# Second attention of a Perceiver kernel by pairs of positions, with a transposed down projection and another order of loads

## The reference

```
x += xattn0(ln(x), ctx, bias)        # 16 heads of 16, over 1024 keys, then a GELU MLP
x += delta_memory(ln(x))             # chunked recurrence with a 64x64 inverse
x += sum over 8 experts of silu(x Wg) * (x Wu) @ Wd
x += xattn1(ln(x), ctx)              # below
x += attn1(ln(x))                    # 16 heads of 16 within the 64 positions
x += top-1 of 8 relu experts
```

```
q = x @ Wq; k, v = split(context @ Wkv)
mask = (j % n_q == i)                # n_q = 64 positions: key j counts only for query j % 64
attn = softmax(where(mask, q k^T / 8, -max))
out = (attn @ v) @ Wout + bout
```

## Time and profile before

| what | value |
|---|---|
| median of 3 executions | 916.06 us |
| the profiled execution's own time | 919.98 us |
| its span (first to last instruction) | 918.2 us |
| mean granted clock | 0.975 |
| TensorE busy | 855.8 us, 93% |
| VectorE busy | 508.3 us, 55% |
| ScalarE busy | 412.6 us, 45% |
| GpSimd busy | 105.6 us, 12% |
| DMA | 128.15 MB, 139 GB/s from and to HBM |

### The profile page before, as it was taken

The page is one execution under the profiler, slowest core; times in us unless marked ns, Lnnn a source line. Parts: engine busy times, 40 slices in busy tenths (PEclk is TensorE's granted clock), DMA queues, the critical chain, the costliest instruction groups (busy, mean ns, idle before and its releaser), DMA issues.

```text
span 918.2 us, 20804 instructions
## 1 busy us (share of the span) xinstructions
PE 855.8 (93%) x8290; PEld 709.5 (77%) x8290; DVE 508.3 (55%) x1182; ACT 412.6 (45%) x820; POOL 105.6 (12%) x102
## 2 busy tenths in 40 slices
PE   5999999999799799999999999999989999659997
PEld 3788888888657787888888888884489957547786
DVE  4778887787616646555555555544366504734232
ACT  3666666666631224545454545442456522401221
POOL 2333332130000700000000000000011003100100
PEclk9999999999999899999999999999999999778999
DMA  8446664464360000302312321009046594040960
GB/s 301 174 154 204 226 221 179 173 203 152 132 259 0 3 4 0 138 18 121 138 51 87 137 88 49 0 0 353 13 145 267 184 380 171 2 185 14 372 260 24
DMA packets 25868, 128.15 MB, mean 140 GB/s; under 512 B 2360, under 2 KB 8272, under 8 KB 21712
## 3 DMA queue, kind: packets, MB, share of 16 engines
q1 hardware_dynamic: 24624, 111.51, 32.6%
q0 software_dynamic: 1184, 15.77, 4.4%
HBM read 126.75 MB, written 0.52 MB: 139 GB/s over the span
## 4 chain that ended last, share of the span: by engine, by line
PE 85%; DVE 7%; DMA 3%; issue 2%; ACT 2%; SPq 0%; DVEq 0%; ACTq 0%
PE PS L387 13%; PE PS L388 13%; PE PS L389 13%; PE PS L698 5%; PE PS L396 4%; PE PS L940 4%; PE PS L1142 3%; PE PS L821 3%; PE PS L959 3%; PE PS L710 3%; PE PS L687 3%; PE PS L1154 3%; DMA arena<-in_bias 2%; PE PS L928 2%; PE PS L913 2%
## 5 line engine op out<-in xcount | busy, mean ns | idle before, releaser
L1679 DVE TENSOR_TENSOR w_l<-arena,w_h 128x768 fp32r<-128x768 f32 x64 | 61.2, 957 | 91.6 <-ACT w_h L1322 91.6
L1322 ACT CAST w_h<-arena 128x768 fp32r<-128x768 f32 x64 | 53.4, 836 | 129.2 <-PE PS L389 129.2
L387 PE MATMUL PS<-xnT_h,w_h 128*128 128x512 f32 x256 | 100.5, 393 | 0.8 <-DVE xnT_l L381 0.8
L388 PE MATMUL PS<-xnT_l,w_h 128*128 128x512 f32 x256 | 100.3, 392 | 0.0
L389 PE MATMUL PS<-xnT_h,w_l 128*128 128x512 f32 x256 | 99.6, 389 | 0.0
L1517 DVE CUSTOM_DVE_ANT_0 arena<-PS,arena 128x512 f32<-128x512 f32 x128 | 86.7, 714 | 19.6 <-PE PS L687 17.9
L1222 ACT ACTIVATE arena<-arena 128x1024 f32<-128x1024 f32 x64 | 73.5, 1151 | 10.7 <-DVE arena L1517 10.6
L389 PE MATMUL PS<-w_h,h_l 128*128 128x256 f32 x256 | 72.4, 283 | 0.0
L388 PE MATMUL PS<-w_l,h_h 128*128 128x256 f32 x256 | 72.4, 283 | 0.0
L387 PE MATMUL PS<-w_h,h_h 128*128 128x256 f32 x256 | 72.1, 282 | 0.0
L698 PE MATMUL PS<-consts,arena 128*128 128x128 f32 x512 | 68.3, 277 | 0.7 <-ACT arena L1227 0.4
(11 more groups left out here) (297 smaller groups left out, 1832.1 us busy)
## 6 DMA issues: line engine op xcount, KB each, us to landing
arena<-in_bias SPq DMA_DIRECT2D x64, 512.0 KB, 4.1
arena<-in_wall SPq DMA_DIRECT2D x8, 3072.0 KB, 10.2
arena<-in_wf SPq DMA_DIRECT2D x8, 2052.0 KB, 11.4
hT<-in_ctxT SPq DMA_DIRECT2D x12, 1024.0 KB, 6.5
arena<-in_ctxT SPq DMA_DIRECT2D x4, 1024.0 KB, 6.4
arena<-in_ctxG SPq DMA_DIRECT2D x4, 1024.0 KB, 4.8
hT<-in_ctxG SPq DMA_DIRECT2D x4, 1024.0 KB, 4.8
arena<-in_w SPq DMA_DIRECT2D x2, 1024.0 KB, 6.3
```

The source lines that it names most:

```text
L387: pe.matmul(out, a[0], b[0], start=start, stop=False)
L388: pe.matmul(out, a[0], b[1], start=False, stop=False)
L1322: act.copy(w_h[:, s % 4, :], stage[s // 8 % 2][:, s % 8, :]).then_inc(sem("c_wh"), 1)
L1679: dve.tensor_tensor(w_l[:, s % 4, :], stage[s // 8 % 2][:, s % 8, :], wide(w_h[:, s % 4, :]), ALU.subtract).then_inc(sem("c_wl"), 1)
```

## The change

Three parts.

1. **Second attention two positions at a time.** U becomes `U[dc]` = [batch x pair of positions, 2 x 16 heads], so a pair's 32 columns lie side by side. Scores of a pair are [32 columns] x [32 keys], placed in one of four 32-column groups of the array; 4 pairs in parallel groups, 8 such steps fill [128, 256] of one bank. The regrouping copies go. DVE adds the constant "pair" (0 or -1e30), takes the maximum and subtracts it for all 8 steps at once, ACT takes one exponential, DVE sums and normalises. Two transposes instead of eight. The sums run on 32-row groups, one per pair, each into a bank of its own (4 to 7). Scores and sums of a batch have two buffers in PSUM where they had halves, the results' banks have one. Loops over batches are written out.
2. **Down projection of the first layer's experts turned around.** The weights are the stationary operand, the result is channels x tokens in banks 4 and 5; DVE and ACT copy it to `aT`, TensorE transposes it into banks 6 and 7, and DVE adds it.
3. **SP queue.** wq1, wkT1 and wv1 are loaded during the experts; wqkv, wproj and the second layer's experts 0 to 4 together after L982's last product (`d_o`); wrt and b2f ahead of experts 6 and 7. The context in the new layouts `ctxD` and `ctxG` is loaded in the order T, G for each batch; T of batch b waits for the scores of b - 2, G for the sums of b - 2, as before.

More of the change, by code:

```diff
@@ L46, in const_layout @@
         "half2": ((p % 32) // DK == np.arange(2)[None, :]),
-        "group": np.where(p % GI == c % GI, 0.0, -BIG),
+        "pair": np.where(p % 2 == np.arange(32)[None, :] % 2, 0.0, -BIG),
         "upper": i > j,
@@ L464, in _ @@
             sp.wait_ge(sem("a2_o"), 2)
-            with sp.Fori(0, NEXP // 2) as i:
+            for e2 in range(2):
+                sp.dma_start(stage[e2], A["wall"][e2:e2 + 1].rearrange("a p c n -> p (a c) n"))\
+                  .then_inc(sem(f"c_w{e2}"), 16)
+            with sp.Fori(1, NEXP // 2) as i:
                 for e2 in range(2):
@@ L476, in _ @@
             w_in(wv1, A["wv1"], "in_wvo1")
+            sp.wait_ge(sem("c_dn"), 4 + 8 * NEXP)
             w_in(wo1, A["wo1"], "in_wvo1")
[L478 to L490, removed]
+            for b in range(B):
+                if b >= 2:
+                    sp.wait_ge(sem("d_sim"), b - 1)
+                sp.dma_start(ctxT1[b % 2], A["ctxD"][b].rearrange("(k p) n -> p k n", p=P))\
+                  .then_inc(sem(f"d_ctxT{b % 2}"), 16)
+                if b >= 2:
+                    sp.wait_ge(sem("d_w"), b - 1)
+                sp.dma_start(ctxG[b % 2], A["ctxG"][b]).then_inc(sem(f"d_ctxG{b % 2}"), 16)
+            sp.wait_ge(sem("d_o"), FC)
             w_in(wqkv, A["wqkv"], "in_wqkv")
@@ L495, in expert_in @@
                 sp.dma_start(wblk[e], A["wf"][e * P:(e + 1) * P]).then_inc(sem(f"f_w{e // 2}"), 16)
[L497 to L501, removed]
+            for e in range(5):
                 expert_in(e)
@@ L929, in _ @@
                                   start=True, stop=True).then_inc(sem(f"d_u{dc}"), 1)
[L931 to L955, removed]
-                    for dc in range(KC):
[L957 to L962, removed]
@@ L1362, in exps @@
             def exps(b):
-                for hf in range(2):
-                    act.wait_ge(sem("d_z"), b * 2 + hf + 3)
-                    for g in range(4):
-                        last = act.activation(Z[:, hf, g, :], Z[:, hf, g, :], ACT.Exp, bias=mx1[:, hf, g:g + 1],
-                                              scale=-1.0, accum_out=rs1[:, hf, g:g + 1])
-                    last.then_inc(sem("d_e"), 1)
+                act.wait_ge(sem("d_z"), b + 1)
+                z = Z[:, b % 2].rearrange("p a b -> p (a b)")
@@ L1370, in transposed @@
+                act.activation(z, z, ACT.Exp).then_inc(sem("d_e"), 1)
             def transposed(b):
[L1371 to L1373 removed]
+                act.wait_ge(sem("d_t"), b + 1)
+                act.copy(PTx[:, b % 2].rearrange("p a b -> p (a b)"), PS[:, 2 + b % 2, 0:2 * P])\
+                   .then_inc(sem("d_te"), 1)
@@ L1375, in summed @@
             def summed(b):
-                for hf in range(2):
-                    act.wait_ge(sem("d_w"), b * 4 + hf * 2 + 7)
-                    act.copy(U[:, 1, :, bass.ds(b * S + hf * 32, 32)].rearrange("p h (g i) -> p g h i", g=4),
-                             PS[:, 5 + 2 * hf, :].rearrange("p (g h i) -> p g h i", g=4, h=XH))\
-                       .then_inc(sem("d_we1"), 1)
-            exps(0)
-            with act.Fori(1, B) as b:
-                transposed(b - 1)
-                exps(b)
-                summed(b - 1)
@@ L1387, in _ @@
-            transposed(B - 1)
-            summed(B - 1)
+                act.wait_ge(sem("d_w"), b + 1)
+                for dc in range(KC):
+                    last = act.copy(U[dc][:, b * PP + 16:(b + 1) * PP, :].rearrange("p (r q) n -> p r (q n)", r=2),
+                                    PS[:, 6:8, dc * D:(dc + 1) * D])
+                last.then_inc(sem("d_we1"), 1)
+            exps(0)
+            for b in range(B):
+                transposed(b)
+                if b + 1 < B:
+                    exps(b + 1)
+                summed(b)
@@ L1700, in _ @@
             dve.wait_ge(sem("c_dn"), 4 + 8 * NEXP)
-            for t in range(NT):
-                ch.add(dve.tensor_tensor(x_tok[:, t, :], PS[:, 4 + t, 0:D], x_tok[:, t, :], ALU.add))
+            dve.tensor_copy(aT[:, 0], bank(4)).then_inc(sem("c_turn"), 1)
+            for i in range(2):
+                dve.wait_ge(sem("c_y"), i + 1)
+                ch.step(dve.tensor_tensor(two(x_tok, i), bank(6 + i), two(x_tok, i), ALU.add))
+                ln_stats(dve, ch, x_tok, (2 * i, 2 * i + 1))
             ch.sync()
             dve.sem_inc(sem("x_tok"), 1)
-            ln_stats(dve, ch, x_tok, range(NT))
             ln_dve(dve, ch, 6, x_tok, xn_tok, sem("tr_src"))
@@ L1751, in _ @@
             scores(0)
-            grouped(1)
             probabilities(0)
-            with dve.Fori(1, B - 1) as b:
-                ch.enter(b - 1, 2)
-                scores(b)
-                grouped(b + 1)
-                probabilities(b)
-                summed(b - 1)
-                ch.leave(B - 2)
-            scores(B - 1)
-            probabilities(B - 1)
-            summed(B - 2)
-            summed(B - 1)
+            for b in range(B):
+                if b + 1 < B:
+                    scores(b + 1)
+                    probabilities(b + 1)
+                summed(b)
```

116 lines of the change are left out of this document (40 added, 76 removed).

## The result

The changed kernel takes 924.05 us (median of 6, 919.12 to 927.42) against 914.34 for the kernel before (median of 6): ratio 1.0105, interval 1.0069 to 1.014. Run once more beside the last experiments it was 918.14 against 914.15, ratio 1.0048, interval 1.0026 to 1.0071. It is slower, by half to one per cent; the forecast was faster by 3%.

What follows compares the result with a forecast made beforehand. TensorE, busy 93% of the span, was taken to bound the kernel. Terms -3.5 + 2.4 - 16.1 - 13.8 = -31.0 from the median of 916.06 gave 885 us; own range 878 to 892, wider range 871 to 914.

Steps and rivals of the forecast that it cites:

- the attention's round: Second attention, TensorE's time per batch: scores 2.1, transposes and handovers 1.2, sums 3.6, tiling change 0.1; 7.0 us against 8.5.
- the serial rival: Second attention's sums: row groups load weights one after another, 14.3 us instead of 3.6; kernel 970 us, chance 0.05.
- The rival had the falling clock: Second attention's loop: clock falls to 1.2 GHz for few columns in flight and pauses; round 11.1, kernel 914 us, chance 0.14.
- Instruction supply: Second attention's scores: supply of instructions sets the time, 2.1 us for 128 records.
- The rival had it as a slower rate: Second attention's scores: slower instruction supply, 3.5 us, round 8.4; kernel 895 us, chance 0.15.
- the second 7.2 us after the trigger: Second attention's context loads: ctxT, queued behind ctxG, lands 7.2 us after sums end and gates scores one round later.
- The rule (7.0 + 7.2)/2: Second attention: round is the larger of TensorE's 7.0 us and the mean with the transfers' 7.2, so 7.1 us.
- Pair reading in the `wv1` products: Products after the second attention: reading the moving operand in pairs costs 0; bounds 0 and 13.97 us.
- The rival of halved speed (+14): Products with `wv1`: pairs halve TensorE's read, + 14 us; kernel 899 us, chance 0.08.
- Down projection: First layer's expert blocks: 6 records of 512 columns replace 12 of 256, -3.5 us over 64 blocks; bounds 0 and -7.
- The transposes behind it: After the experts' last product: copies and transposes before the adds and statistics, 5.3 us against 2.96, +2.4 us.
- Router: Router: early input loads remove waiting, -8.2 us, and the clock stays at 1.0, 5.6 us more; -13.8 in all.

Runs made afterwards that it cites:

- fill: Changed kernel plus unused full-array matmuls in the second attention, 2 or 6 a batch: 920.54 us (2) and 915.63 us (6).
- wide resident loop: Changed kernel, 128 columns streamed in sums, up to 64 in scores, transposes ahead of next scores, six middle batches as a two-batch loop: 892.98 us, ratio 0.978.
- no pauses: Changed kernel with each batch's transposes issued ahead of the next batch's scores: 916.11 us, ratio 1.0015 to the kernel before.
- narrow: Changed kernel, 32 columns streamed, transposes ahead of next scores, TensorE's six middle batches as a two-batch loop: 908.08 us, ratio 0.9932 to the kernel before.
- wide without pauses: Changed kernel, sums streaming 128 columns and scores up to 64 instead of 32, transposes ahead of next scores: 909.03 us, ratio 0.9946 to the kernel before.
- the last kernel: The wide resident loop with ctxT of batch b + 1 issued ahead of ctxG of batch b: 885.70 us, ratio 0.9695 to the kernel before.
- attention undone: Changed kernel's projection and router order, with the attention, contexts and loads of the kernel before: 894.02 us, ratio 0.9774.

## Why the prediction was wrong

**The step that failed** is the attention's round, "2.1 + 1.2 + 3.6 + 0.1 = 7.0 us against 8.5". It took sums of 3.6 us from rows at 2.4 GHz and left the clock at 1.0. The size is right for that clock: 3.84 with fill, 3.75 to 3.77 in the wide resident loop, so the four row groups do load side by side (the serial rival is excluded). At the granted 0.5 they take 7.05 or more, and the sums of the eight batches are 26 of the 31.6 us by which the loop missed. Another 4 us went before the first sums, 10.3 us behind the first scores where 6.0 was forecast, with a stop of 2.57 us in them.

The rival had the falling clock and even the size of a round (11.1 against 10.7 to 11.6). Of its two reasons one stands, the few columns in flight; the pauses that it named as well are not needed for it. I gave it 0.14 because "small-tile matmuls without pause kept 1.00" from 313 to 333. That row is another kind of matmul, 692 records of 64x64 tiles with 64 columns streamed, and "no pauses" shows that pauses are not the point: TensorE without one stays at 0.50, and comes up once each instruction drives more columns (0.84) or full-array work stands between (0.82). The narrow and the wide resident loop differ in nothing but the columns streamed, and have 0.59 and 0.89. I should have asked how much work each instruction puts into the array, not how busy the engine is called. That this is how the chip decides isn't shown; the runs show which streams were held down and which came up.

On that, the Trainium skill (TensorE: Matmul & The Clock Gate, "Why this matters for your kernels") advises to leave no long idle gaps between bursts of matmuls. By this case's runs that is not enough: "no pauses" has none of more than about half a microsecond from 667 us on and stays at 1.2 GHz.

**Instruction supply.** I priced it as a rate: 2.1 us for 128 scores, from L1019. As a rate that was high, it is 1.82 (0.0142 a record; at the low clock 1.75 for 116, 0.0151, so the clock hardly sets it). The rival had it as a slower rate, 3.5 us; it has the rate wrong, but supply does cost, as stops of some 2 us at every 512 instructions. In the changed kernel they are short (0.3 to 1.1 us a batch), as is to be expected where the low clock slows what uses the instructions up. With the clock up they are the next limit: wide without pauses, with a clock of 0.84, is at 909.

The Trainium skill (Runtime: NRT & Kernel Launch, "Instruction fetch mechanics") has the 16 KB blocks of 256 instructions that the trace shows, and holds that their fetch is hidden since the sequencer dispatches more slowly than it fills; it prefers full unrolling, because a taken branch can break the prefetch. Here an unrolled stream of small matmuls is stopped all the same, and a loop of two batches is 15 us faster (wide: 0.9946 to 0.978).

**Transfers.** "the second 7.2 us after the trigger" is right (6.8 to 6.9 to land, plus issue). The rule (7.0 + 7.2)/2 was hidden by the slow round. In the wide resident kernel, whose TensorE round is 5.9, it gives (5.9 + 7.2)/2 = 6.55, and the chain has scores waiting for ctxT at 697.89 and, two batches on, at 710.88: 6.5 us a batch. The other order of the queue removes it.

**Pair reading in the `wv1` products.** Forecast 0 loss. At full clock the 64 records take 15.79 us, with fill and in the last kernel alike, against 13.97: +1.8 us, 13%. In the changed kernel it is 17.40, since the clock is back only at about 759; that is the other 1.6 of the stage's +3.4. The rival of halved speed (+14) is out. The pairs are what the change does to these products, and the loads that ran beside them before are gone; no run undoes the pairs alone. The Trainium skill (SBUF — State Buffer, "Door 1: The DMA port swizzle") has full bandwidth from two accesses to a 16-byte line on, and also a penalty, of no stated size, at each step to a new line; the prediction took the first half alone. Measured, pairs are 13% slower.

**Down projection.** -3.5 forecast, -6.3 measured; right in kind. After, the six records of a block step by 0.2265 us:

```profile
...
512.63 0.39 PE L386 MATMUL PS<-h_h,w_h 128*128 128x512 f32 x1
...
513.99 0.39 PE L386 MATMUL PS<-xnT_h,w_h 128*128 128x512 f32 x1
...
516.71 0.39 PE L386 MATMUL PS<-h_h,w_h 128*128 128x512 f32 x1
...
```

They take 1.36 us where 12 took 1.43, and the gate and up products 2.72 where 2.75 was: 0.10 x 64 = 6.4. I had counted the saving on the down part alone. The transposes behind it cost +1.9, forecast +2.4. The last record of the products starts at 622.57; the copy, the first add and the last statistics follow:

```profile
...
622.99 0.69 DVE L1677 COPY aT<-PS 128x512 f32<-128x512 f32 x1 [1.94 <-PE PS L388]
...
624.89 0.69 DVE L1680 TENSOR_TENSOR x_tok<-PS,x_tok 128x512 f32<-128x512 f32 x1 [1.20 <-PE PS L878]
...
626.99 0.75 DVE L317 BATCH_NORM_STATS2 small<-x_tok 128x6 f32<-128x256 f32 x2
...
```

From the copy to the end of the statistics 4.75 us; forecast were 5.3 with 0.1 ahead of it, before it was 2.96.

**Router.** -8.2 and -5.6 forecast, -6.8 to -8.3 and -5.7 measured. Not forecast were -4.6 at the end: before, TensorE stops in the L1142 blocks for 0.34 to 0.38 us at a time, as here, and these stops are gone in every kernel with the new order, also where that order is the only edit.

```profile
...
847.61 0.39 PE PS L1142 x6
848.00 0.34 issue
848.34 0.39 PE PS L1142 x6
848.73 0.34 issue
...
```

What makes them isn't shown.

**Before the experts.** Their first product starts at 352.9 us in the profile of before and 361.5 after, but 357.8 in the changed kernel's second profile and 351.5 to 355.7 in the experiments that kept the new contexts and have the same code up to there. (The expectation of "attention undone" reads this start some 3 us later, at 356 and 365.) So the 8.6 us are no certain cost of the change. In the chain up to there, the landing of a bias tile (`in_bias`, 512 KB) stands twice before, 15.8 us in all, and six times in both profiles of the changed kernel, 48 us; in the kernel "wide, no pauses", which starts at 351.5, three times. Why these loads are waited for more often isn't shown.

The sum: parts 2 and 3 gave what was forecast and 5 us more (894.02 against a forecast of 899 for them alone, 914.34 - 3.5 + 2.4 - 13.8), and part 1 turned from -16 into +19 in its own stages (query stage, loop and `wv1` products), +25 to +30 with the later start before the experts. That the last kernel comes to 885.70, the number once forecast for the changed one, is in part luck: its loop takes 63.5 us where 60.2 was forecast and its `wv1` products 1.8 more, and the end of the kernel, where nothing was forecast, gives 4.6 back.

## What to carry to other kernels

Price a matmul on small tiles at both clock levels, and ask how much of the array each instruction moves, not whether the engine is busy: if it is little, stream more columns where they are free rather than fewer, and read the granted clock again. When instructions get shorter and more, count them against the stops that every 512 of them brought here, and keep the loop short enough to be repeated. Then look at which load stands behind which wait on its queue: a small load behind big ones cost 14 us here, and a context load behind a wait that it didn't need 7 us.

## What was not expected of the hardware

- The granted clock stayed at 0.51 over 84 us with TensorE busy 88% of the time, nearly all of it small tiles.
- Sums on 32 rows x 128 columns take 0.030 us a record with 32 columns streamed (1.92 for 64) and as much with up to 128 (3.75 for 128): the further columns cost nothing, as if hidden behind the weight loads. At the low clock 32 columns take 0.055.
- Scores of 32 columns, four column groups, take 0.0142 us a record at 2.4 GHz and 0.0151 at 1.2.
- An unrolled stream at the high clock stopped 1.9 to 2.8 us at every second 16 KB of instructions; a loop of two batches fetched none in 15 us.
- Moving operands in runs of two fp32 took 15.79 us for 64 records against 13.97 in contiguous runs.
